# The prologue of an attention and feed-forward kernel: scale of A from a bound by row sizes, Wv loaded apart, first x-hat rounded directly, first z by kinds of products

## The reference, cut to what matters

```python
# x: [16, 1024, 256]; W_qkv: [768, 256]; w_gate, w_up: int32 [768, 256]; w_down: int32 [256, 768]
def _L0_attn_ref(t, W_qkv, b_qkv):
    qkv = jnp.einsum('bnd,ed->bne', t, W_qkv) + b_qkv
    Q, K, V = qkv[:, :, :256], qkv[:, :, 256:512], qkv[:, :, 512:]
    scores = jnp.einsum('bqd,bkd->bqk', Q, K) / jnp.sqrt(jnp.float32(256))
    attn = jax.nn.softmax(scores, axis=-1)
    return jnp.einsum('bqk,bkv->bqv', attn, V)
def _L0_ffn_ref(x, w_gate, w_up, w_down):          # wg, wu, wd = w_* / 127
    h = jax.nn.silu(x @ wg.T) * (x @ wu.T)
    return h @ wd.T
x = x + _layernorm(_L0_attn_ref(_layernorm(x), W_qkv, b_qkv))
x = x + _layernorm(_L0_ffn_ref(_layernorm(x), w_gate, w_up, w_down))
```

## Time and profile before

| | us |
|---|---|
| median of 3 runs | 1379.21 (1378.70 to 1379.24) |
| the profiled execution | 1381.24 |
| its span in the profile | 1379.5 |
| TensorE busy in the span | 1351.6 (98%) |
| VectorE, ScalarE, POOL busy | 897.8, 877.6, 823.2 |
| mean granted TensorE clock | 0.993 |

### The profile page before, as it was taken

One profiled execution on the slowest core, in us unless ns is written; L12 is line 12 of the kernel. 1 busy time (PEld: TensorE's weight loads), 2 busy tenths in 40 slices (PEclk: granted clock), 3 DMA queues, 4 the chain that ended last, 5 costly groups with the idle time before them and its releaser, 6 DMA issues.

```text
span 1379.5 us, 22293 instructions
## 1 busy us (share of the span) xinstructions
PE 1351.6 (98%) x7369; PEld 723.5 (52%) x7369; DVE 897.8 (65%) x2160; ACT 877.6 (64%) x1373; POOL 823.2 (60%) x1002
## 2 busy tenths in 40 slices
PE   8898999999999999999999999999999999999987
PEld 4354555554555545555554555545555555555544
DVE  6776666766657666666666657667666666647565
ACT  4657575675766567575675767567575774756544
POOL 2668376483846658376484756748376484745544
PEclk9999999999999999999999999999999999999999
DMA  7987392753827456373753836447383663716311
GB/s 198 189 170 161 54 165 68 133 133 70 160 78 136 109 101 137 92 153 70 134 142 70 160 78 126 119 96 142 84 155 77 122 139 83 132 60 117 92 39 48
DMA packets 437176, 158.29 MB, mean 115 GB/s; under 512 B 418113, under 2 KB 420417, under 8 KB 437058
## 3 DMA queue, kind: packets, MB, share of 16 engines
q1 hardware_dynamic: 436272, 156.03, 54.5%
q10 hardware_dynamic: 786, 0.79, 0.2%
HBM read 36.70 MB, written 16.78 MB: 39 GB/s over the span
## 4 chain that ended last, share of the span: by engine, by line
PE 90%; DVE 3%; issue 2%; POOL 1%; SPq 1%; DMA 1%; ACT 1%; ACTq 0%; POOLq 0%
PE S L710 90%; DMA yTl<-yl 1%; SPq L245 1%; DVE mxs L613 1%; DVE S L642 1%; DVE st L651 0%; POOL rs L293 0%; PE S L729 0%; POOL Pl L338 0%; POOL yl L365 0%; DVE st L669 0%; DVE X L664 0%; SPq L226 0%; SPq L251 0%; DVE hf L679 0%
## 5 line engine op out<-in xcount | busy, mean ns | idle before, releaser
L438 ACT ACTIVATE P<-S,nmx,sc 128x1024 f32<-128x1024 f32 x128 | 153.7, 1201 | 287.0 <-DVE nmx L617 286.9
L613 DVE TENSOR_REDUCE mxs<-S 128x1 f32<-128x1024 f32 x128 | 156.1, 1220 | 126.7 <-PE S L710 126.3
L679 DVE SCALAR_TENSOR_TENSOR hf<-S,sc,hf 128x512 f32<-128x512 f32 x192 | 141.9, 746 | 140.8 <-ACT hf L473 133.8
L338 POOL TENSOR_TENSOR Pl<-P,Ph 128x1024 f16<-128x1024 f32 x96 | 204.4, 2130 | 38.6 <-issue 26.4
L710 PE MATMUL S<-xTh,zTh 128*128 128x512 f16 x512 | 195.2, 381 | 4.5 <-ACT P L438 2.2
L710 PE MATMUL S<-PTh,xh 128*128 128x512 f16 x512 | 194.4, 380 | 1.0 <-DVE hf L679 1.0
L710 PE MATMUL S<-xTl,zTh 128*128 128x512 f16 x512 | 195.2, 381 | 0.0
L710 PE MATMUL S<-xTh,zTl 128*128 128x512 f16 x512 | 195.2, 381 | 0.0
L710 PE MATMUL S<-PTl,xh 128*128 128x512 f16 x512 | 194.4, 380 | 0.0
L710 PE MATMUL S<-PTh,xl 128*128 128x512 f16 x512 | 194.2, 379 | 0.0
L289 POOL TENSOR_SCALAR rs<-mv,sc 128x2 f32<-128x2 f32 (+1 forms) x96 | 35.2, 366 | 233.2 <-DVE mv L655 191.7
(11 more groups left out here) (115 smaller groups left out, 2463.6 us busy)
## 6 DMA issues: line engine op xcount, KB each, us to landing
xs<-in_L_attn_t SPq DMA_DIRECT2D x32, 512.0 KB, 5.4
X<-in_L_attn_t SPq DMA_DIRECT2D x32, 512.0 KB, 4.5
out_x<-X SPq DMA_DIRECT2D x64, 256.0 KB, 2.9
PTh<-Ph SPq DMA_TRANSPOSE x128, 3.2
PTl<-Pl SPq DMA_TRANSPOSE x128, 3.2
hTh<-in_L_attn_W_qkv ACTq DMA_DIRECT2D x1, 768.0 KB, 7.1
hTl<-in_L_ffn_w_gate SPq DMA_DIRECT2D x1, 768.0 KB, 7.2
hTh<-in_L_ffn_w_up SPq DMA_DIRECT2D x1, 768.0 KB, 9.0
```

What stands on the lines that cost most here:

```text
L338: p.engine.tensor_tensor(out=Pl[:, m % 3, :], in0=P[:, m % 2, :], in1=Ph[:, m % 3, :], op=ALU.subtract).then_inc(pl_vector if i in PL_ON_V ...
L438: a.engine.activation(P[:, m % 2, :], ps[:, bank:bank + 2, :].rearrange("p a n -> p (a n)"), ACT.Exp, bias=nmx[:, c:c + 1], scale=sS, accu ...
L613: v.engine.tensor_reduce(mxs[:, c:c + 1], ps[:, bank:bank + 2, :].rearrange("p a n -> p (a n)"), axis=AX.X, op=ALU.max, negate=True).then_ ...
L679: v.engine.scalar_tensor_tensor(out=hf[:, n % 3, :], in0=ps[:, bank + 1, :], scalar=sc2[:, 4:5], in1=hf[:, n % 3, :], op0=ALU.mult, op1=AL ...
```

## The change

Four things are changed, all before the first score product.
- The scale of A is no longer made from the largest element of the finished A but from a bound: the sum over all rows e of max|Wq[e]| times max|Wk[e]|, the query bias added to the first with a factor. `row_sizes` makes the row maxima, `sum_rows(0)` on TensorE sums them over the partitions (with a matrix of ones, so that all partitions get the sum), and `bound(0)` makes the power of two and its inverse. `V_row_sizes`, `sum_rows(1)` and `bound(1)` do the same for V. `turn_max`, `powers` and `spread_powers` stay for the feed-forward weights alone. `attention_scales`, as before one step, now stands behind `bound(1)`.
- W_qkv comes in two transfers, Wq and Wk first, Wv second.
- In batch 0 ScalarE makes xh straight from x (four activations a half, `x_first_high`); the x-hat in 32 bits, needed for xl only, is made beside it, into the free tile P: half 0 by VectorE (`x_hat_vector`), half 1 by POOL (`x_hat_pool`).
- `first_z` takes the kinds one after the other: half 0 high, low x, low A; half 1 high, low A, low x; each kind waits only for its own operands. The high transposes of batch 0 get semaphores of their own.

TensorE's 13 `keep_busy` products behind `A_product` become 14 in one group.

```diff
 def load_weights(a):
     a.engine.dma_start(b1, b_d.rearrange("(a n) -> a n", a=1)).then_inc(bias_in, 16)
-    a.engine.dma_start(wq_s, wqkv_d.rearrange("(c p) d -> p c d", p=128)).then_inc(wqkv_in, 16)
+    rows = wqkv_d.rearrange("(c p) d -> p c d", p=128)
+    a.engine.dma_start(wq_s[:, 0:4, :], rows[:, 0:4, :]).then_inc(wqk_in, 16)
+    a.engine.dma_start(wq_s[:, 4:6, :], rows[:, 4:6, :]).then_inc(wv_in, 16)
...
+def x_first_high(a, g):
+    a.wait_ge(nb1_done, g + 1)
+    for t in range(4 * g, 4 * g + 4):
+        done = a.engine.activation(xh[0][:, t, :], xs[:, t, :], ACT.Identity, bias=nb1[:, t:t + 1], scale=rs1[:, t:t + 1])
+    done.then_inc(xh_done, 1)
...
+def row_sizes(v):
+    v.wait_ge(wqk_in, 16)
+    for dst, c in ((rq, 0), (rk, 2)):
+        v.engine.tensor_reduce(dst[:, :], wq_s[:, c:c + 2, :], axis=AX.X, op=ALU.max, apply_absolute_value=True
+                               ).then_inc(v_step, 1)
...
+    v.engine.scalar_tensor_tensor(out=rq[:, :], in0=bqa[:, :], scalar=2.0 ** -10, in1=rq[:, :], op0=ALU.mult, op1=ALU.add)
+    v.engine.tensor_tensor(out=rq[:, :], in0=rq[:, :], in1=rk[:, :], op=ALU.mult).then_inc(row_size[0], 1)
+
+def V_row_sizes(v):
+    v.wait_ge(wv_in, 16)
+    abs_max(v, 1, wq_s[:, 4:6, :]).then_inc(row_size[1], 1)
+
+def bound(v, n):
+    v.wait_ge(bound_out[n], 1)
+    v.engine.tensor_scalar(size[:, n:n + 1], pb_[:, 8 + n:9 + n], scalar1=2.0 ** -100, scalar2=None, op0=ALU.max)
+    v.engine.tensor_scalar(pow2[:, n:n + 1].bitcast(i32), size[:, n:n + 1].bitcast(i32), scalar1=0x7F800000, scalar2=None,
+                           op0=ALU.bitwise_and).then_inc(v_step, 1)
+    v.engine.reciprocal(size[:, n:n + 1], pow2[:, n:n + 1]).then_inc(v_step, 1)
+
+def x_hat_vector(v, b, g):
+    v.wait_ge(nb1_done, 2 * b + g + 1)
+    for t in range(4 * g, 4 * g + 4):
+        v.engine.tensor_scalar(x_hat_at(b, t), xs[:, t, :], scalar1=rs1[:, t:t + 1], scalar2=nb1[:, t:t + 1],
+                               op0=ALU.mult, op1=ALU.add).then_inc(xn_vector, 1)
...
+def sum_rows(t, n):
+    t.wait_ge(const_done, 4)
+    t.wait_ge(row_size[n], 1)
+    if n:
+        t.wait_ge(sA_ready, 1)
+    out = pb_[:, 8 + n:9 + n]
+    if n:
+        t.engine.matmul(out, ones, am[:, 1:2], start=True, stop=True).then_inc(bound_out[1], 1)
+    else:
+        t.engine.matmul(out, ones, rq[:, 0:1], start=True, stop=False)
+        t.engine.matmul(out, ones, rq[:, 1:2], start=False, stop=True).then_inc(bound_out[0], 1)
...
+def first_z(t, g, bank, late):
+    high, low_x, low_A = ((Ah, xTh, 0), (Ah, xTl, 1), (Al, xTh, 2))
+    if g:
+        t.wait_ge(w_lo, 1)
+    kinds = (high, low_x, low_A) if late == 2 else (high, low_A, low_x)
+    for a, x, kind in kinds:
+        if kind == 0:
+            t.wait_ge(w_hi, 1)
+            t.wait_ge(x0_turned[g], 16)
+        elif kind == 1:
+            t.wait_ge(x_turned[g], 16)
+        else:
+            t.wait_ge(w_lo, 1)
+        for dj in range(2):
+            for di in range(2):
+                done = t.engine.matmul(cols(ps[:, bank + dj, :]), a[:, di, dj * 128:(dj + 1) * 128],
+                                       x[0][:, 4 * g:4 * g + 4, di, :], start=(kind == 0 and di == 0),
+                                       stop=(kind == late and di == 1))
+            if kind == late:
+                done.then_inc(z_done, 1)
...
 # GpSimd
 x_norm(p, 0, 1)
+x_hat_pool(p, 0, 1)
 x_norm(p, 1, 0)
...
 # ScalarE
 load_weights(a)
-x_hat(a, 0, 0)
-x_high(a, 0, 0)
-x_hat(a, 0, 1)
-x_high(a, 0, 1)
+x_first_high(a, 0)
+x_first_high(a, 1)
 A_high(a)
...
 # VectorE
 x_stats(v, 0, 1)
-V_max(v)
-c_max(v)
-A_max(v)
+row_sizes(v)
+x_hat_vector(v, 0, 0)
 x_low(v, 0, 0)
-powers(v, 0, 2, pb_, 2.0 ** -100, 1)
+bound(v, 0)
 scale_A(v)
 x_low(v, 0, 1)
 A_low(v)
+V_row_sizes(v)
+bound(v, 1)
 attention_scales(v)
 V_low(v)
...
 # TensorE
 c_product(t)
+sum_rows(t, 0)
 A_product(t)
-keep_busy(t, 2, const_done, 3)
-turn_max(t, 0, 2, pb_, 2)
-keep_busy(t, 3, const_done, 3)
-spread_powers(t, 0, 2, pb_, 1)
-keep_busy(t, 8, const_done, 3)
-project_z(t, 0, 0, 0, (w_lo, 1), (w_lo, 1))
-project_z(t, 0, 1, 2, (w_lo, 1), (w_lo, 1))
+keep_busy(t, 14, const_done, 3)
+first_z(t, 0, 0, 2)
+first_z(t, 1, 2, 1)
+sum_rows(t, 1)
 score(t, 0, 0, 4, None, None)
```

More of the change, by code:

```diff
@@ L17 @@
 HL_ON_VECTOR = (2, 5)
-XN_ON_POOL = ((1, 1), (2, 1))
+XN_ON_VECTOR = ((0, 0),)
+XN_ON_POOL = ((0, 1), (1, 1), (2, 1))
 class Lane:
@@ L86, in sandwich @@
         am = sb("am", [128, 9])
+        rq, rk, bqa = sb("rq", [128, 2]), sb("rk", [128, 2]), sb("bqa", [128, 2])
+        size, pow2 = sb("size", [128, 2]), sb("pow2", [128, 2])
         ax = sb("ax", [1, 6])
@@ L111, in sems @@
             return [sem(f"{name}{i}") for i in range(n)]
-        bias_in, wqkv_in = sem("bias_in"), sem("wqkv_in")
+        bias_in, wqk_in, wv_in = sem("bias_in"), sem("wqk_in"), sem("wv_in")
         ffn_in = sems("ffn_in", 3)
@@ L117, in sandwich @@
         xs_in, x_turned, X_in = sems("xs_in", 2), sems("x_turned", 2), sems("X_in", 4)
+        x0_turned = sems("x0_turned", 2)
         p_turned, y_turned, stored = sems("p_turned", 3), sem("y_turned"), sems("stored", 4)
@@ L121, in sandwich @@
         max_turned, powers_out = sem("max_turned"), sem("powers_out")
+        bound_out = sems("bound_out", 2)
         z_done, S_done, Y_done = sem("z_done"), sem("S_done"), sem("Y_done")
@@ L159, in sandwich @@
         b1 = flat(ft)[0:1, 0:3 * D]
-        pa = ps[:, 0:2, 0:D]
+        pa = ps[:, 2:4, 0:D]
         pb_, pc_ = OB[0], OB[1]
@@ L163, in sandwich @@
         fv = half_words(yn, 1024)
+        ones = flat(PTh[0]).bitcast(f32)[:, 0:128]
         stage = ((half_words(X[0], 1536), half_words(X[1], 1536)), (half_words(X[2], 1536), half_words(X[3], 1536)),
@@ L191, in xn_wait @@
                 e.wait_ge(xn_pool, 4 * XN_ON_POOL.index((b, g)) + 4)
+            elif (b, g) in XN_ON_VECTOR:
+                e.wait_ge(xn_vector, 4)
             else:
-                e.wait_ge(xn_done, 4 * (2 * b + g + 1 - sum(k < (b, g) for k in XN_ON_POOL)))
+                e.wait_ge(xn_done, 4 * (2 * b + g + 1 - sum(k < (b, g) for k in XN_ON_POOL + XN_ON_VECTOR)))
         def xl_wait(e, b, g):
@@ L220, in turn_x @@
             src, dst = ((xh, xTh), (xl, xTl))[low]
+            done = x_turned[g] if b or low else x0_turned[g]
             if low:
@@ L226, in turn_x @@
             s.engine.dma_start_transpose(dst[k][:, gs, :, :].rearrange("p t d n -> p (t d) n"),
-                                         src[k][:, gs, :].rearrange("p t d -> p (t d)")).then_inc(x_turned[g], 16)
+                                         src[k][:, gs, :].rearrange("p t d -> p (t d)")).then_inc(done, 16)
         def reload(s, b, g):
@@ L285, in constants @@
             p.engine.memset(mhalf[:, :], -0.5).then_inc(const_done, 1)
+            p.engine.memset(ones, 1.0).then_inc(const_done, 1)
         def inv_std(p, rs, var, eps, mul=None):
@@ L304, in x_norm @@
                 xn_wait(p, b - 1, g)
+                p.wait_ge(xh_done, 2 * b + g - 1)
             inv_std(p, rs1[:, gs], mv1[:, gs, 1], EPS, XS ** -2).then_inc(g_step, 1)
@@ L307, in x_norm, with x_hat_at @@
             neg_mean(p, nb1[:, gs], mv1[:, gs, 0], rs1[:, gs]).then_inc(nb1_done, 1)
+        def x_hat_at(b, t):
+            return xs[:, t, :] if b else P[:, t // 4, (t % 4) * D:(t % 4) * D + D]
         def x_hat_pool(p, b, g):
@@ L319, in x_low @@
             pv_wait(p, b - 2, 1)
-            p.engine.tensor_tensor(out=xl[k][:, gs, :], in0=xs[:, gs, :], in1=xh[k][:, gs, :], op=ALU.subtract
+            src = xs[:, gs, :] if b else P[:, g, :].rearrange("p (t d) -> p t d", d=D)
+            p.engine.tensor_tensor(out=xl[k][:, gs, :], in0=src, in1=xh[k][:, gs, :], op=ALU.subtract
                                    ).then_inc(xl_done if b else xl0_done, 1)
@@ L402, in V_high @@
         def V_high(a):
-            a.wait_ge(wqkv_in, 16)
+            a.wait_ge(wv_in, 16)
             a.wait_ge(attn_scaled, 5)
@@ L516, in A_max @@
-        def A_max(v):
-            v.wait_ge(A_ready, 1)
-            abs_max(v, 0, pa).then_inc(v_step, 1)
-            v.wait_ge(v_step, v.tick(v_step))
-            v.engine.tensor_tensor(out=am[:, 0:1], in0=am[:, 0:1], in1=am[:, 5:6], op=ALU.max).then_inc(max_ready, 1)
+            v.wait_ge(bq_copied, 1)
+            v.engine.tensor_reduce(bqa[:, :], bq[:, :].rearrange("p (c n) -> p c n", n=1), axis=AX.X, op=ALU.max,
+                                   apply_absolute_value=True).then_inc(v_step, 1)
@@ new lines, in copy_bq @@
+            v.tick(v_step)
+        def row_sizes(v):
[3 more added lines that the diff above has]
+                                       ).then_inc(v_step, 1)
+                v.tick(v_step)
+            v.wait_ge(v_step, v.told[v_step.name])
+            v.engine.scalar_tensor_tensor(out=rq[:, :], in0=bqa[:, :], scalar=2.0 ** -10, in1=rq[:, :], op0=ALU.mult, op1=ALU.add
+                                          ).then_inc(v_step, 1)
+            v.wait_ge(v_step, v.tick(v_step))
```

(38 more changed lines are left out.)

13 lines of the change are left out of this document (3 added, 10 removed).

## The result

The changed kernel takes 1384.41 us (median of 6, 1382.69 to 1386.31) against 1379.22 of before, measured beside it: a ratio of 1.0037, 95% interval 1.0026 to 1.0048, 5.2 us slower. Measured again on another occasion it was 1383.25 against 1379.81, 1.0031 (1.0018 to 1.0044), 3.4 us slower. In us the two intervals are 3.6 to 6.6 and 2.5 to 6.1. The forecast was 1383.2, 4.0 slower or a ratio of 1.0029, inside both.

What follows compares the result with a forecast made beforehand. TensorE, busy 98% of the span, was taken as the bound, so only the prologue's shift counts: -3.2 for z, +5.3 serial chain, +1.9 clock, +4.0 us in all, from 1379.21 to 1383.2; 8 in 10 range 1379.7 to 1385.6.

Steps and rivals of the forecast that it cites:

- `x_hat_vector`, each: VectorE's x-hat for half 0 in the prologue: four operations of 256 elements, 0.35 us each, bounds 0.15 to 0.48.
- xTl of the first half lands: Transpose of the low x for the first z's first half: lands 3.2 us after its issue, at 15.75.
- POOL's x-hat: Half 1's x-hat on POOL from 10.43: four operations at 0.547, done at 12.7; even at 4.18 it costs nothing.
- from there to the first score: Serial chain from z's last slot through `sum_rows(1)`, bound, scales and z rounding to score: 5.7 us instead of 0.4, +5.3.
- clock, at the first row maximum: Half clock after TensorE's 5.4 us idle ahead of score slows the first score product: +1.9 us, at most 2.5.
- The gain: Prologue up to the end of the first z: z ends at 20.1 instead of 23.29, 3.2 us earlier.
- the rival of a first z at half clock: First z at half clock, or its inputs late: +5.7 us, 1384.9; chance 0.15.
- The loss: Behind the first z: `sum_rows(1)` queued after both `first_z` makes score start at 25.8 instead of 23.71, 2.1 us later.
- the 3.98 and the 2.19 of the forecast: TensorE idle stretches in the earlier trace: 3.98 us left the clock at 0.50, 2.19 did not lower it.
- The signs of being wrong: Score before 24.6, clock staying at 1.00, or the first row maximum's difference gone at 100 us would refute the forecast.
- the rival in which falls of before are spared: Two later clock falls, near 50 and 1330 us, costing 3.0 and 2.2, don't recur: -1.2 us, 1378.0; chance 0.12.
- three runs of before within 0.6 us: Argument against the spared falls: the agreement of these runs speaks for clock falls that come with the idle stretch.

Runs made afterwards that it cites:

- changed, again: The changed kernel with no edit, measured once more on another occasion: 1383.25 against 1379.81, ratio 1.0031.
- pure delay: Kernel before with 40 filler products on TensorE between the first z and the first score, nothing else of the change: 1382.17 against 1379.42, ratio 1.0022.
- 66 fillers: Changed kernel with 66 filler products behind the second sum over rows, outlasting TensorE's new wait: 1382.47, ratio 1.0020.
- 44 fillers: Changed kernel with 44 filler products behind the second sum over rows, in TensorE's new wait: 1379.23, ratio 1.0005.
- sum between: Changed kernel with `sum_rows(1)` ahead of the second half of the first z instead of behind it: 1377.83, ratio 0.9993.
- sum inside: Changed kernel with `sum_rows(1)` inside the first z's first half, behind its high products, and V's row sizes ahead of VectorE's second low x: 1375.23, ratio 0.9969.
- sum inside, fillers: The kernel with V's sum inside the first half of z, plus 8 and 10 filler products around the feed-forward maxima's transposes (44 to 48 us): 1375.53, ratio 0.9974.
- the transfer of the weights: Changed kernel with all query, key and value weights in one 768 KB transfer again, nothing else changed: one execution, 1383.98.

## Why the prediction was right

By its own steps, as the changed kernel's profile shows them:

| step | forecast | measured |
|---|---|---|
| `x_hat_vector`, each | 0.35 | 0.345 (four in 1.38) |
| xTl of the first half lands | 15.75 | 15.8 |
| first z product starts | 14.05 | 14.18 |
| last slot of the z products ends | 20.1 | 20.19 |
| POOL's x-hat | 2.2, once 4.18; hidden | 3.13; VectorE waits 0.96, TensorE not |
| from there to the first score | 5.7 | 5.56 |
| first score product | 25.8 | 25.75 |
| clock, at the first row maximum | 1.9 | 2.3 |
| pause of before that falls away | 0 | 0.36 |
| delay at the second row maximum | 4.0 | 3.95 |

The measured terms add up as the forecast's do: -3.1 for z, +5.14 for the serial chain (5.56 instead of 0.42), +2.27 for the clock, -0.36 for the pause. Part of the closeness is luck. The clock cost 0.4 more than the 1.9 taken, and the pause, which the sum didn't know of, gave nearly as much back. xTl landed on time because VectorE's x-hat began 0.24 early (9.61 for 9.85) while its low x took 0.16 longer than the 1.23 taken. And the first median lay 1.2 above this delay, which its interval allows.

**The gain** is real and is thrown away: z ends 3.1 earlier than before (20.19 against 23.29). Of that, 0.7 is half clock: before, the granted clock was 0.50 until 18.9, over the first z products, and here it was 1.00 from 9.9 to 23.6, so that the rival of a first z at half clock didn't come true. **The loss** is where it was put, in TensorE's queue order; moving one line by one place gained 2.8 at the score, and into z's own wait 4.75. **The clock** fell in the new wait of 5.28, in all three profiles that have it, and held in one of 2.67, between the 3.98 and the 2.19 of the forecast; the fillers showed its price directly. The bounds aren't firm, though: it also fell in a wait of 2.95 (at 112 us, above), and in one profile of ten behind the wait of 2.19. The Trainium skill's rule (TensorE: Matmul & The Clock Gate, section on HAM oscillation), that idle stretches put the array back to half rate, agrees with 5.28. The Trainium skill's rule of two elements a cycle (VectorE: DVE Perf Modes, section on mode 2x_2P) does not: 256 elements from SBUF to SBUF took 0.345, and 0.2 was the estimate by it. POOL's x-hat isn't the reason, as the changed kernel's timeline shows:

```profile
9.61 1.38 DVE L567 TENSOR_SCALAR P<-xs,rs,nb 128x256 f32<-128x256 f32 x4
...
10.85 3.13 POOL L328 TENSOR_SCALAR P<-xs,rs,nb 128x256 f32<-128x256 f32 x4
11.09 1.39 DVE L337 TENSOR_TENSOR xl<-P,xh 128x1024 f16<-128x1024 f32 x1
```

Three of the four were over when POOL's began, and all four have the same duration, 0.41 each (they overlap a little). ScalarE's activations on SBUF ran beside them throughout.

**The signs of being wrong.** The score didn't start before 24.6 and the clock didn't stay at 1.00. The third sign, that the difference at the first row maximum is no longer there at 100 us, came half true: 2.49 of 4.31 was left. The pause took 0.36 of it. The other 1.46 went near 50 us, where before has 6.8 us of half clock and the changed kernel 3.4, as in the rival in which falls of before are spared; in the first profile 3.1 came back at 112 us, in the second not.

**The argument that failed** is a side one: that three runs of before within 0.6 us speak for falls of the clock that come with the idle stretch. The 28 and 24 executions of before taken beside the experiments run from 1376.5 to 1381.9, and the idle stretch near 50 us brought 6.8, 3.4 or no us of half clock in different profiles. The profile of before used for the sum was one with the long fall, in an execution of 1381.24.

**Delays and medians.** Over before, in us:

| version | delay, row maxima 2 to 7 | median | interval |
|---|---|---|---|
| changed | 3.95 | 5.2 | 3.6 to 6.6 |
| changed, again | 3.97 | 3.4 | 2.5 to 6.1 |
| pure delay | 3.75 | 2.75 | 1.7 to 4.3 |
| 66 fillers | 3.37 | 2.7 | 1.4 to 4.1 |
| 44 fillers | 1.52 | -0.2 | -0.6 to 1.8 |
| sum between | -1.1 | -1.6 | -2.3 to 0.3 |
| sum inside | -3.1 | -4.2 | -5.9 to -2.8 |
| sum inside, fillers | -3.0 | -4.3 | -5.0 to -2.1 |

Every interval holds its delay. So nothing here needs another cause than the delay, and the 1.2 by which the first median lies above it isn't told from noise.

**What is open.** No run takes the four changes apart, apart from the transfer of the weights, so how much of z's 3.1 each of them gives isn't shown. Most medians lie on the low side of their delays; these share their executions of before, and whether there is more in it isn't shown. Falls of the clock at about 50, 101, 112 and 1330 us, and the landing of transposes, differ from one execution to the next by 1 to 3 us. The four profiles of kernels with extra fillers had no fall near 50 us, the six without had one. Three of those four had their fillers 20 us ahead of it, and why that should matter was not found.

## What to carry to other kernels

A producer's order on one engine can cost more than the producer itself: a product of 0.3 us behind 24 others made VectorE wait 3.94 and ScalarE 7.66 us, and then TensorE 5.28, because each of them had its next needed step queued behind something that hung on it. When a step is taken off the front of a queue, look for what now stands last ahead of the next phase, and put small products that feed scales into waits that the engine has anyway. Sum the delay at the first point from which one engine runs without a break, and check it there by the start times of a repeated instruction; the median of a kernel whose clock falls here and there followed that delay here only to within one or two us.

## What was not expected of the hardware

POOL's four operations of 256 elements took 3.13, and 2.2 or 4.18 in the kernel before. The excess of the 3.13 is in one of them, which took 1.50 from 11.41 on, beside VectorE's low x with its two inputs from SBUF; the three others took 0.55 each. That low x took 1.39, and the second one, when POOL's were done, 1.22.

A stretch of half clock began 23.6 us into the span in the changed kernel and lasted into the score; equal idle stretches at 50 us were followed by 6.8, 3.4 or no us of it, and one of 2.2 near 100 us by 3.4 us of it in one profile of ten. And a wait of 0.74 ahead of `A_product` was, in that one execution, followed by 3.4 us of half clock that nearly doubled its time.
